# Attention scores on 32-row strips of TensorE with 0/1-masked keys, in a two-layer cross-attention and mixture-of-experts kernel

## The chip, the cores and the metric

The kernel runs on one core of a Trainium2 chip. A core has TensorE (PE: matmuls on an array of 128 rows by 128 columns; its loads of weights are shown apart, as PEld), VectorE (DVE), ScalarE (ACT), GpSimd (POOL), SyncE (SP, which here only issues DMAs), and 16 DMA engines. The metric is the device time of one execution in microseconds, as the median of three runs.

## The reference

The input x has 16 sequences of 128 tokens with 256 features; the context ctx has the same shape. Two layers follow each other, each an attention over the context and a mixture of experts, with a LayerNorm ahead of each:

```python
x = x + xattn0(layernorm(x), ctx)            # 16 heads of 16 features, rotary positions on q and k
x = x + ffn0(layernorm(x))                   # top 2 of 8 experts, and a shared one
x = x + xattn1(layernorm(x), ctx, mask)      # 16 heads of 16 features, padding mask on keys
x = x + ffn1(layernorm(x))                   # top 4 of 16 experts by groups, and a shared one
# each attention, for a sequence and a head h:
#   scores = q_h @ k_h.T / 4                 [128 x 128], contracted over 16 features
#   out_h  = softmax(scores (+ mask)) @ v_h
# then out = concat(out_h) @ Wo.T + bo
```

## The kernel before, in words

**Precision.** Products that must be accurate are made in three matmuls: each operand is split in a high and a low part (names with _hi and _lo, or index 0 and 1 in `k_parts` and `q_parts`), and hi x hi, lo x hi and hi x lo are summed in PSUM. ACT writes the high part as a rounded copy; DVE writes the low part as the value less its high part.

**Blocks.** Attention works on blocks `n` of four sequences (512 tokens), four blocks a layer. Within a block there are 16 groups of four heads: group i = (sequence b, g) with g from 0 to 3. All 16 groups go through one pipeline.

- PE, `scores` (L1341 to L1343, and L1348 for the mask in layer 1): 128 queries by 4 x 128 scores of a group, in one bank of PSUM. Bank g holds group g of a sequence.
- DVE, `shifted`: `nmax` (L1036), the negated maximum of each head's row, and for even g the subtraction (L1039) that makes `prob`. ACT: exp, L638 for even g from `prob`, L642 for odd g from the bank with `nmax` as bias, four instructions.
- PE, `turned` (L1358): four transposes of the probabilities. ACT `probT_hi` (L660), DVE `probT_lo` (L1065) split them.
- PE, `weighed` (L1373): probabilities times values, two parts. A column of ones beside the values gives the sums. DVE `rden` (L1045) inverts them, ACT `o_raw` (L650) copies the sums out of the bank, POOL (L461, L463, L466) adds the parts and multiplies by `rden` into `o_sb`. DVE does this for the last of a block (`last_outputs`).
- Ends of blocks: oT transposes (L1397), their split (ACT L674, DVE L1078), the products with Wo, and DVE's sum into `xres` (L1088).

The order is written out by hand: on PE, step i is scores(i+4), then turned(i), then weighed(i-2). In the last four steps of a block, where no scores are left, PE makes instead the projection units of the next block (`unit`, L1178): two of keys and two of queries, each 128 features by 512 tokens. Behind the steps PE makes the values of the next block, the oT transposes, the first four groups of scores of the next block, and the products with Wo. In layer 0 a unit goes on through DVE (L1009, twice: times cosine and times sine, with the bias), POOL `rotate` (L451), ACT (L624, high part) and DVE (`unit_low`, L1019, low part). In layer 1 it goes through ACT (L619, bias and scale), ACT (L624) and DVE (L1019). A unit needs the buffer `qk` that the unit two before it gives free.

**The keys.** A matmul here contracts over all 128 rows of the array, and a head has only 16 features. So the right-hand operand is `kexp`, a block-diagonal copy of the keys. It is 128 rows by four heads by 128 keys, where the rows of head j hold its keys in the columns of head j, and all else is zero. POOL sets it to zero once a layer, and SP's queue fills it in every block with small DMAs, of which each copies the 16 rows of a head. There are two buffers of `kexp`, used in turn by sequences:

```python
for g2 in range(2):
    for j in range(GRP):
        rows = slice(64 * g2 + HD * j, 64 * g2 + HD * (j + 1))
        src = k_parts[rows, :, :, b * S:(b + 1) * S]
        dst = kexp[b % 2][rows, :, g2::2, j, :]
        sp.dma_start(dst.bitcast(F32), src.bitcast(F32)).then_inc(a[f"kdma{b % 2}"], 16)
```

That is 8 DMAs a sequence, 32 a block, 256 in the program. SP issues them in order with the loads of the context; behind the last of layer 0 stand the fill of the sorted rows with zeros (L289, `sorted_x`, and L292, `summed`), and the loads of the expert weights (L295, `w_raw`), which POOL (L342) and others split.

The loops over blocks on PE and SP are hardware loops (`Fori`) over the first three blocks, with the fourth written out behind them.

## Time and profile before

| | |
|---|---|
| time, median of 3 runs | 1128.84 us (1124.97 to 1131.86) |
| span of the profiled execution | 1130.6 us; no time apart from it is given for that execution |
| PE busy | 990.0 us, 88% |
| DVE busy | 789.2 us, 70% |
| ACT busy | 588.3 us, 52% |
| POOL busy | 453.7 us, 40% |
| attention of layer 0 | from about 50 to 248 us |
| LayerNorm between attention and experts of layer 0 | 249 to 274 us |
| attention of layer 1 | 617 to 786 us |

The profile is of one execution. Busy shares are averages over stages with different limits, so they say where to look and not what sets the time. The chain of waits says that: it is followed back from the last instruction to what released each step. In a row with an idle time in brackets, the engine stood idle for so long before that instruction, and what is named released it.

### The profile page before, as it was taken

To read this page: it belongs to the slowest core of one execution; us is meant where nothing else is said; L and a number is where in the kernel's file an instruction comes from. 1 tells how busy PE (TensorE), PEld (TensorE's weight loads), DVE (VectorE), ACT (ScalarE), POOL (GpSimd) and SP (SyncE) were. 2 spreads that over 40 slices of the span, in tenths; PEclk is the share of its full clock that TensorE was granted. 3 is DMA by queue.
4 is the path that set the end of the run, shared out by engine and by line. 5 is a ranking of instruction groups with operands and counts; after the bars stand their busy time and mean duration, and the time that the engine had idled before them with its cause. 6 is when DMAs were issued, how large, how long until landed. Compare 5 with 4: busy or idle time off the path is not lost.

```text
span 1130.6 us, 20561 instructions
## 1 busy us (share of the span) xinstructions
PE 990.0 (88%) x6789; PEld 851.5 (75%) x6789; DVE 789.2 (70%) x1553; ACT 588.3 (52%) x1128; POOL 453.7 (40%) x481
## 2 busy tenths in 40 slices
PE   3798988957988999999946999995889999999995
PEld 2577776844868999999944777774678888888885
DVE  5587777856745677777746887885596766666665
ACT  5384655655423676666637877875622232232221
POOL 4384344424374566666651745342112112212210
PEclk9998989977989999999976999997799999999998
DMA  3311010291223788888760111010001000000002
GB/s 130 89 39 29 28 36 12 64 288 45 80 90 131 216 224 237 233 228 225 194 155 18 39 51 29 15 37 30 28 15 29 14 28 28 14 28 28 14 1 75
DMA packets 64609, 93.00 MB, mean 82 GB/s; under 512 B 8241, under 2 KB 51505, under 8 KB 64561
## 3 DMA queue, kind: packets, MB, share of 16 engines
q0 software_dynamic: 14784, 46.44, 14.8%
q1 hardware_dynamic: 49778, 45.97, 14.4%
q8 instruction: 25, 0.41, 0.2%
q14 instruction: 22, 0.18, 0.1%
HBM read 63.21 MB, written 20.79 MB: 74 GB/s over the span
## 4 chain that ended last, share of the span: by engine, by line
PE 46%; DVE 18%; ACT 13%; issue 10%; DMA 8%; POOL 3%; SPq 1%; ACTq 0%; DVEq 0%; POOLq 0%
PE bank L1178 28%; PE bank L1214 10%; DMA w_raw<-in_fw,w_idx 5%; DVE nmax L1036 4%; DVE probT_lo L1065 2%; DMA summed<-y_sb,tile_to 2%; DVE prob L1039 2%; PE bank L1273 2%; ACT probT_hi L660 2%; ACT xn L522 2%; ACT o_raw L650 2%; POOL qk L451 1%; POOL summed L404 1%; ACT w_hi L543 1%; DVE xres L957 1%
## 5 line engine op out<-in xcount | busy, mean ns | idle before, releaser
L1178 PE MATMUL bank<-xT_hi,w_hi 128*128 128x512 f32 x352 | 140.0, 398 | 3.2 <-DVE hid L970 2.2
L591 ACT ACTIVATE act_sb<-bank 128x512 f32<-128x512 f32 x88 | 52.6, 597 | 173.4 <-PE bank L1178 162.3
L1178 PE MATMUL bank<-xT_hi,w_lo 128*128 128x512 f32 x352 | 139.8, 397 | 1.7 <-issue 1.5
L1178 PE MATMUL bank<-xT_lo,w_hi 128*128 128x512 f32 x352 | 139.8, 397 | 1.1 <-issue 1.1
L970 DVE TENSOR_TENSOR hid<-bank,act_sb 128x512 f32<-128x512 f32 x88 | 60.8, 691 | 113.2 <-ACT act_sb L591 100.6
L342 POOL TENSOR_TENSOR w_hi<-w_raw,zero_col 128x768 fp32r<-128x768 f32 (+1 forms) x20 | 31.9, 1596 | 266.4 <-PE bank L1214 235.8
L957 DVE SCALAR_TENSOR_TENSOR xres<-bank,gate,xres 128x256 f32<-128x256 f32 x320 | 132.5, 475 | 0.8 <-PE bank L1214 0.8
L1178 PE MATMUL bank<-xsT_hi,w_hi 128*128 128x256 f32 x368 | 107.3, 291 | 2.3 <-DVE xsT_lo L924 1.5
L1214 PE MATMUL bank<-w_hi,hid_hi 128*128 128x256 f32 x352 | 100.0, 284 | 6.3 <-DVE hid_lo L978 6.2
L1065 DVE TENSOR_TENSOR probT_lo<-bank,probT_hi 128x512 f16<-128x512 f32 x128 | 87.9, 686 | 23.9 <-ACT probT_hi L660 23.2
L1178 PE MATMUL bank<-xsT_hi,w_lo 128*128 128x256 f32 x368 | 104.0, 283 | 0.0
L1178 PE MATMUL bank<-xsT_lo,w_hi 128*128 128x256 f32 x368 | 103.9, 282 | 0.0
L596 ACT ACTIVATE hid_hi<-hid 128x512 fp32r<-128x512 f32 x88 | 55.6, 632 | 91.9 <-PE bank L1214 53.7
L1214 PE MATMUL bank<-w_hi,hid_lo 128*128 128x256 f32 x352 | 99.2, 282 | 0.0
L1214 PE MATMUL bank<-w_lo,hid_hi 128*128 128x256 f32 x352 | 98.9, 281 | 0.0
L1358 PE MATMUL bank<-ident,prob 128*128 128x128 f32 x512 | 80.2, 280 | 14.4 <-ACT prob L638 7.7
L404 POOL DMA_INDIRECT summed<-y_sb,tile_to x46 | 83.9, 1824 | 21.5 <-DMA summed<-y_sb,tile_to 11.0
L1358 PEld LDWEIGHTS bank<-ident,prob 128*128 128x128 f32 x512 | 60.7, 143 | 37.6 <-ACT prob L638 20.8
L1036 DVE TENSOR_REDUCE nmax<-bank 128x4 f32<-128x512 f32 x128 | 85.5, 674 | 3.0 <-PE bank L1348 2.7
L369 POOL DMA_INDIRECT w_raw<-in_fw,w_idx x46 | 49.8, 1083 | 93.7 <-ACT y_sb L560 29.8
L543 ACT ACTIVATE w_hi<-w_raw 128x1536 fp32r<-128x1536 f32 x46 | 68.1, 1483 | 34.2 <-DMA w_raw<-in_fw,w_idx 33.9
L919 DVE TENSOR_TENSOR w_lo<-w_raw,w_hi 128x1536 fp32r<-128x1536 f32 x46 | 80.6, 1752 | 2.1 <-issue 1.4
(204 smaller groups left out, 2957.4 us busy)
## 6 DMA issues: line engine op xcount, KB each, us to landing
kexp<-k_parts SPq DMA_DIRECT2D x256, 32.0 KB, 2.0
w_raw<-in_fw SPq DMA_DIRECT2D x18, 384.0 KB, 3.0
sorted_x<-empty_row SPq DMA_DIRECT2D x2, 2967.0 KB, 20.6
xs<-sorted_x SPq DMA_DIRECT2D x23, 258.0 KB, 3.9
ctx_raw<-in_ctxT SPq DMA_DIRECT2D x8, 512.0 KB, 4.2
aw_raw<-in_aw SPq DMA_DIRECT2D x10, 256.0 KB, 3.2
summed<-empty_row SPq DMA_DIRECT2D x1, 2304.0 KB, 25.9
xres<-in_x SPq DMA_DIRECT2D x4, 512.0 KB, 6.2
```

What stands on the lines that cost most here:

```text
L404: nc.gpsimd.indirect_dma_start(out=summed, out_offset=bass.IndirectOffsetOnAxis(ap=tile_to[:, j, c:c + 1], axis=0), in_=y_sb[:, j % 2, c, ...
L543: nc.scalar.activation(w_hi4[s][:], w_raw4[s], ACT.Copy).then_inc(TS["w_hi"], 1)
L591: nc.scalar.activation(act_sb[:, (ls * J + j) % 2, :], bank[2 * ((ls * J + j) % 2) + 1][:], ACT.Silu).then_inc(f["act"], 1)
L596: nc.scalar.activation(hid_hi[:, ls % 2, j, :], hid[:, (ls * J + j) % 2, :], ACT.Copy).then_inc(f["hhi"], 1)
L919: nc.vector.tensor_tensor(w_lo4[s][:], w_raw4[s], w_hi4[s][:].bitcast(F32), ALU.subtract).then_inc(TS["w_lo"], 1)
L957: nc.vector.scalar_tensor_tensor(out=rows, in0=bank[4 + 2 * (ls % 2) + sub // 2][:, D * (sub % 2):D * (sub % 2 + 1)], scalar=gate[:, ds(it ...
L970: nc.vector.tensor_tensor(hid[:, r, :], bank[2 * r][:], act_sb[:, r, :], ALU.mult).then_inc(f["hid"], 1)
L1036: nc.vector.tensor_reduce(mx, grp, AX.X, ALU.max, negate=True).then_inc(a["max"], 1)
L1065: nc.vector.tensor_tensor(probT_lo[:, i % RINGT, :], bank[4 + i % 2][:], probT_hi[:, i % RINGT, :], ALU.subtract).then_inc(a["plo"], 1)
L1178: last = nc.tensor.matmul(dst, lh, rh, start=(i == 0), stop=(i == len(pairs) - 1))
L1214: last = nc.tensor.matmul(dst, h, w, start=(i == 0), stop=(i == len(pairs) - 1))
L1358: last = nc.tensor.transpose(bank[4 + i % 2][:, S * h:S * (h + 1)], prob[:, i % RING, S * h:S * (h + 1)], ident[:])
```

## The change

- `kexp`, its DMAs and its zeroing go. A tile `gap` stands in the place of `kexp`, so that the tiles behind it keep their addresses.
- `k_parts` holds each key unit twice for each part: once times `half_col[:, 0]` and once times `half_col[:, 1]`. `half_col` is 1 in the first or in the second 16 rows of every 32, and 0 elsewhere. DVE makes it once from the identity matrix. ACT and DVE thus write two copies of high and low part for each of two key units a block. The counts of the semaphores `qkhi` and `qklo` go from 4 to 6 a block.
- `scores` takes two groups at a time, g and g+1. A strip of 32 rows holds two heads of each of the two feature tiles u. A matmul contracts over the 32 rows of strip r, and its right-hand operand is the two masked copies side by side (256 columns). Bank r gets 256 columns for u = 0 and 256 for u = 1. Matmuls on the two strips alternate. The pair waits for the subtraction and the exp of the groups whose banks it writes.
- The heads of a group are now 8u + 2g + j; `weighed`, the outputs and `last_outputs` address them so (`four_by_two`).
- In layer 1 the mask is added by four matmuls of 256 columns over 32 rows, so `mask_b` and `first_row` stand on all strips. The DMA of the mask writes 128 partitions (1 MB) instead of one (8 KB).
- The `Fori` loops over blocks on PE and SP become Python loops, which are unrolled.

```diff
-        k_parts = sb(at, "k_parts", [P, 2, KT, N], F32R)
-
-        kexp = [sb(at, f"kexp{i}", [P, 2, NG, GRP, S], F32R) for i in range(2)]
+        k_parts = sb(at, "k_parts", [P, 2, KT, 2, N], F32R)
+        gap = sb(at, "gap", [P, 6 * 1024], F32)
...
-                sp.dma_start(mask_f, maskrow).then_inc(s_in, 16)
+                sp.dma_start(mask_f, maskrow.to_broadcast([P, TOK])).then_inc(s_in, 16)
...
-                with sp.Fori(0, NBLK - 1) as n:
+                for n in range(NBLK - 1):
                     sp.wait_ge(a["ctx_lo"], n + 1)
-                    sp.dma_start(ctx_raw[:], ctxT[:, :, ds(n * N + N, N)]).then_inc(a["ctx_in"], 16)
-                    keys(n)
-                keys(NBLK - 1)
+                    sp.dma_start(ctx_raw[:], ctxT[:, :, n * N + N:n * N + 2 * N]).then_inc(a["ctx_in"], 16)
...
-                    dst = k_parts if i < 2 else q_parts
-                    nc.scalar.activation(dst[:, 0, i % 2, :], qk[:, i % 2, :], ACT.Copy).then_inc(a["qkhi"], 1)
+                    if i >= 2:
+                        nc.scalar.activation(q_parts[:, 0, i % 2, :], qk[:, i % 2, :], ACT.Copy).then_inc(a["qkhi"], 1)
+                    else:
...
+                        for h in range(2):
+                            nc.scalar.activation(k_parts[:, 0, i, h, :], qk[:, i, :], ACT.Copy,
+                                                 scale=half_col[:, h:h + 1]).then_inc(a["qkhi"], 1)
...
+                    for h in range(2):
+                        dve.wait_ge(a["qkhi"], m * 6 + (2 * i + h + 1))
+                        nc.vector.scalar_tensor_tensor(
+                            out=k_parts[:, 1, r, h, :], in0=qk[:, r, :], scalar=half_col[:, h:h + 1],
+                            in1=k_parts[:, 0, r, h, :].bitcast(F32), op0=ALU.mult,
+                            op1=ALU.subtract).then_inc(a["qklo"], 1)
...
-                    if b >= 1 and g % 2 == 0:
+                    if b >= 1:
                         pe.wait_ge(a["sub"], n * 8 + (i - NG) // 2 + 1)
-                    elif b >= 1:
-                        pe.wait_ge(a["exp"], n * GROUPS + (i - NG + 1))
-                    if g == 0:
-                        pe.wait_ge(a[f"kdma{b % 2}"], n * 256 + (b // 2 + 1) * 128)
-                    q = [q_parts[:, part, g // 2, S * b:S * (b + 1)] for part in range(2)]
-                    k = [kexp[b % 2][:, part, g].rearrange("p h t -> p (h t)") for part in range(2)]
-                    nc.tensor.matmul(bank[g][:], q[0], k[0], start=True, stop=False)
-                    nc.tensor.matmul(bank[g][:], q[1], k[0], start=False, stop=False)
-                    last = nc.tensor.matmul(bank[g][:], q[0], k[1], start=False, stop=(l == 0))
...
+                        pe.wait_ge(a["exp"], n * GROUPS + (i + 1 - NG + 1))
+                    cols = slice(S * b, S * (b + 1))
+                    for u in range(KT):
+                        for part, (pq, pk) in enumerate(((0, 0), (1, 0), (0, 1))):
+                            for r in (g, g + 1):
+                                rows = slice(32 * r, 32 * r + 32)
+                                last = nc.tensor.matmul(bank[r][:, 256 * u:256 * u + 256], q_parts[rows, pq, u, cols],
+                                                        k_parts[rows, pk, u, :, cols], start=(part == 0),
+                                                        stop=(part == 2 and l == 0))
...
+                        if l == 1:
+                            at_tok = slice((n * BLK + b) * S, (n * BLK + b + 1) * S)
+                            for r in (g, g + 1):
+                                rows = slice(32 * r, 32 * r + 32)
+                                row = mask_b[rows, at_tok].unsqueeze(1).to_broadcast([32, 2, S])
...
                     for i in range(GROUPS):
                         if i + NG < GROUPS:
-                            scores(n, i + NG)
+                            if i % 2 == 0:
+                                scores(n, i + NG)
...
-                        for g in range(NG):
+                        for g in range(0, NG, 2):
                             scores(n + 1, g)
...
-                with pe.Fori(0, NBLK - 1) as n:
+                for n in range(NBLK - 1):
                     attend(n, True)
```

## Rows read from the trace of the kernel before

**Rows 1.** The page: busy time by engine, and the chain that ended last.

```profile
PE 990.0 (88%) x6789; PEld 851.5 (75%) x6789; DVE 789.2 (70%) x1553; ACT 588.3 (52%) x1128; POOL 453.7 (40%) x481
...
PE bank L1178 28%; PE bank L1214 10%; DMA w_raw<-in_fw,w_idx 5%; DVE nmax L1036 4%; DVE probT_lo L1065 2%; DMA summed<-y_sb,tile_to 2%; DVE prob L1039 2%; PE bank L1273 2%; ACT probT_hi L660 2%; ACT xn L522 2%; ACT o_raw L650 2%; POOL qk L451 1%; POOL summed L404 1%; ACT w_hi L543 1%; DVE xres L957 1%
```

**Rows 2.** Windows: us, busy of PE, PEld, DVE, ACT, POOL, clock, DMA, GB/s.

```profile
87.60:138.70 51.10, 44.76 (x344) 37.21 (x344) 39.09 (x69) 30.50 (x73) 23.25 (x33) 0.93 0.12 31
645.50:687.10 41.60, 39.61 (x337) 31.04 (x337) 34.28 (x61) 32.99 (x78) 18.23 (x29) 1.00 0.15 38
```

**Rows 3.** Chain of waits in a block of layer 0: start, us, step.

```profile
122.03 0.50 ACT probT_hi L660
...
125.69 0.49 ACT probT_hi L660
```

**Rows 4.** Timeline of PE, then DVE, in the same block of layer 0.

```profile
120.42 0.47 PE L1341 MATMUL bank<-kexp,q_parts 128*128 128x512 f32 x1
...
120.97 0.40 PE L1343 MATMUL bank<-kexp,q_parts 128*128 128x512 f32 x1
...
125.38 0.63 PE L1358 MATMUL bank<-ident,prob 128*128 128x128 f32 x4 [0.38 <-ACT prob L638]
...
123.27 0.64 DVE L1036 TENSOR_REDUCE nmax<-bank 128x4 f32<-128x512 f32 x1
...
126.21 0.69 DVE L1065 TENSOR_TENSOR probT_lo<-bank,probT_hi 128x512 f16<-128x512 f32 x1 [0.38 <-ACT probT_hi L660]
```

**Rows 5.** Timeline of PE, two products of 256 columns in a row.

```profile
104.60 0.28 PE L1178 MATMUL bank<-aw_hi,oT_hi 128*128 128x256 f32 x1
...
104.72 0.28 PE L1178 MATMUL bank<-aw_hi,oT_lo 128*128 128x256 f32 x1
```

**Rows 6.** Timeline of PE, then DVE, at a block's head in layer 1.

```profile
664.08 0.40 PE L1341 MATMUL bank<-kexp,q_parts 128*128 128x512 f32 x1
...
665.20 0.69 DVE L1036 TENSOR_REDUCE nmax<-bank 128x4 f32<-128x512 f32 x1
...
668.41 0.68 DVE L1036 TENSOR_REDUCE nmax<-bank 128x4 f32<-128x512 f32 x1
```

**Rows 7.** Timeline of ACT and DVE at the start of layer 0.

```profile
55.80 1.14 ACT L642 ACTIVATE prob<-bank,nmax 128x128 f32<-128x128 f32 x4
...
57.00 1.28 DVE L1036 TENSOR_REDUCE nmax<-bank 128x4 f32<-128x512 f32 x2
```

**Rows 8.** Timeline of PE and DVE at the start of layer 1.

```profile
622.41 0.50 PE L1341 MATMUL bank<-kexp,q_parts 128*128 128x512 f32 x1 [1.04 <-DMA kexp<-k_parts]
...
623.64 0.69 DVE L1036 TENSOR_REDUCE nmax<-bank 128x4 f32<-128x512 f32 x1 [1.10 <-PE bank L1348]
```

**Rows 9.** Timeline of POOL and DVE in the LayerNorm after attention 0.

```profile
256.78 2.75 POOL L342 TENSOR_TENSOR w_hi<-w_raw,zero_col 128x1536 fp32r<-128x1536 f32 x1 [17.22 <-DMA w_raw<-in_fw]
...
257.40 2.14 DVE L767 SCALAR_TENSOR_TENSOR shift<-meanvar,rstd 128x4 f32<-128x4 f32 x1
```

**Rows 10.** Timeline of DVE in the key units of layer 0.

```profile
134.21 0.69 DVE L1019 TENSOR_TENSOR k_parts<-qk,k_parts 128x512 fp32r<-128x512 f32 x1 [1.47 <-ACT k_parts L624]
134.82 0.75 DVE L1009 SCALAR_TENSOR_TENSOR qk<-bank,bias_col,rope_tab 128x512 f32<-128x512 f32 x1
```

**Rows 11.** Timeline of ACT at the end of a block, layer 1.

```profile
646.59 0.63 ACT L624 ACTIVATE k_parts<-qk 128x512 fp32r<-128x512 f32 x1
647.12 0.49 ACT L650 ACTIVATE o_raw<-bank 128x400 f32<-128x400 f32 x1
...
649.79 0.60 ACT L660 ACTIVATE probT_hi<-bank 128x512 f16<-128x512 f32 x1 [0.28 <-PE bank L1358]
```

**Rows 12.** Windows of 2 us ahead of `values`, columns as in the second group.

```profile
92.00:94.00 2.00, 0.36 (x8) 0.28 (x8) 1.59 (x3) 1.26 (x3) 0.97 (x2) 0.99 0.21 50
94.00:96.00 2.00, 0.92 (x11) 0.93 (x12) 1.13 (x3) 0.00 (x0) 0.72 (x2) 0.50 0.21 49
...
652.00:654.00 2.00, 1.15 (x24) 0.99 (x21) 1.37 (x4) 1.97 (x5) 1.37 (x3) 1.00 0.15 36
```

More of the change, by code:

```diff
@@ L212, in tile_no, with four_by_two @@
             return it * (STEPS * J) + (ls * J + j)
+        def four_by_two(c):
+            return (o_raw[:, c % 2].rearrange("p (u m) w -> p u m w", u=2),
+                    o_sb[:, c // 2].rearrange("p (u c m) d -> p c u m d", u=2, c=2)[:, c % 2])
         block = ctx.enter_context(nc.Block())
@@ L262, in _ @@
                     later_constants()
-                def keys(n):
-                    sp.wait_ge(a["qklo"], n * 4 + 2)
-                    for b in range(BLK):
-                        if b >= 2:
-                            sp.wait_ge(a["score"], n * GROUPS + (b - 1) * NG)
-                        for g2 in range(2):
-                            for j in range(GRP):
-                                rows = slice(64 * g2 + HD * j, 64 * g2 + HD * (j + 1))
-                                src = k_parts[rows, :, :, b * S:(b + 1) * S]
-                                dst = kexp[b % 2][rows, :, g2::2, j, :]
-                                sp.dma_start(dst.bitcast(F32), src.bitcast(F32)).then_inc(a[f"kdma{b % 2}"], 16)
-                sp.wait_ge(a["kzero"], 2)
-                with sp.Fori(0, NBLK - 1) as n:
+                for n in range(NBLK - 1):
                     sp.wait_ge(a["ctx_lo"], n + 1)
-                    sp.dma_start(ctx_raw[:], ctxT[:, :, ds(n * N + N, N)]).then_inc(a["ctx_in"], 16)
-                    keys(n)
-                keys(NBLK - 1)
+                    sp.dma_start(ctx_raw[:], ctxT[:, :, n * N + N:n * N + 2 * N]).then_inc(a["ctx_in"], 16)
                 if l == 0:
@@ L458, in outputs @@
                                 rotate(n + 1, i)
[L459 removed]
+                        raw, dst = four_by_two(c)
                         pool.wait_ge(a["ocopy"], n * 8 + (c + 1))
[L461 removed]
+                        nc.gpsimd.tensor_tensor(dst, raw[:, :, :, 0:16], raw[:, :, :, 18:34], ALU.add).then_inc(a["oadd"], 1)
                         pool.wait_ge(a["oadd"], n * 14 + (2 * c + 1))
[L463 removed]
+                        nc.gpsimd.tensor_tensor(dst, dst, raw[:, :, :, 34:50], ALU.add).then_inc(a["oadd"], 1)
                         pool.wait_ge(a["oadd"], n * 14 + (2 * c + 2))
                         pool.wait_ge(a["rden"], n * 8 + (c + 1))
[L466 removed]
+                        nc.gpsimd.tensor_tensor(dst, dst, rden[:, c % 2].rearrange("p (u m) -> p u m", u=2).unsqueeze(3).to_broadcast([P, 2, 4, HD]),
                                                 ALU.mult).then_inc(a["o"], 1)
                 nc.gpsimd.memset(v_parts[:, :, :, HD:HD + 2], 1.0).then_inc(a["vones"], 1)
[L470 to L471 removed]
                 if l == 0:
@@ L1350, in scores @@
-                    last.then_inc(a["score"], 1)
+                        pe.wait_ge(a["exp"], n * GROUPS + (i + 1 - NG + 1))
[7 more added lines that the diff above has]
+                                                        stop=(part == 2 and l == 0))
+                                if u == KT - 1 and part == 2 and l == 0:
+                                    last.then_inc(a["score"], 1)
+                        if l == 1:
[3 more added lines that the diff above has]
+                                row = mask_b[rows, at_tok].unsqueeze(1).to_broadcast([32, 2, S])
+                                last = nc.tensor.matmul(
+                                    bank[r][:, 256 * u:256 * u + 256].rearrange("p (h t) -> p h t", h=2),
+                                    first_row[rows, :], row, start=False, stop=True)
+                                if u == KT - 1:
+                                    last.then_inc(a["score"], 1)
@@ L1374, in weighed @@
                                                     p[:, i % RINGT, S * h:S * (h + 1)],
-                                                    v_parts[:, b, GRP * g + h, :], start=(part == 0), stop=(part == 1))
+                                                    v_parts[:, b, head, :], start=(part == 0), stop=(part == 1))
                     last.then_inc(a["pv"], 1)
@@ L1431, in _ @@
                     pe.wait_ge(s_vset, 2)
-                pe.wait_ge(s_set, 5)
-                for g in range(NG):
+                pe.wait_ge(s_set, 7)
+                for g in range(0, NG, 2):
                     scores(0, g)
-                with pe.Fori(0, NBLK - 1) as n:
+                for n in range(NBLK - 1):
                     attend(n, True)
```

67 lines of the change are left out of this document (34 added, 33 removed).

## The prediction

> **What bounds the kernel now.** I read the page first, then the two attention loops by windows, then the chain of waits inside one block of each, and last the timelines of PE, DVE, ACT and SP where the change touches them. The page [rows 1] shows PE 88% busy and lines of PE at the head of the chain, and that invites one to expect a gain from faster score matmuls. But most of PE's chain is L1178 and L1214, the FFN, which the change does not touch. What the change is worth must be read inside attention, some 190 us of layer 0 and 170 us of layer 1. A middle block takes 51.1 us in layer 0 and 41.6 us in layer 1 [rows 2].
>
> In the body of a block the chain has no PE step: ACT copies probT_hi, DVE makes probT_lo, rden, nmax and the shifted prob, ACT makes exp and o_raw and copies the next probT_hi. This ring turns once for two groups, from 122.03 to 125.69 [rows 3]: 3.66 us, and the same in layer 1. PE in that time does two score groups, two sets of transposes and two of weighed sums. In layer 0 it then idles 0.38 us before it can transpose, and DVE idles 0.38 us for ACT [rows 4]; a score group takes PE 0.31+0.23+0.23 = 0.77 us. In layer 1 the mask matmul adds 0.23 us and PE is full, though not in the ring. What the change speeds up is thus beside the path.
>
> **Part 1: the scores.** Before, two groups are 6 matmuls of 512 columns: 2 x 0.77 = 1.5 us. After, they are 12 matmuls of 256 columns. A 256-column matmul steps by 0.12 us [rows 5]. If two strips don't overlap at all, a pair takes 12 x 0.12 = 1.4 us; if they overlap fully, 0.7 us. In layer 1 the masks are 2 x 0.23 before and 4 x 0.12 or half of it after: a pair is 1.9 or 0.95 us with them. No row of before shows two strips. I take full overlap (a strip leaves the other rows of the array idle) and keep the other end. In the ring it matters little: the group that PE scores from 120.42 on is read by DVE at 123.27 [rows 4], 2.8 us later, and either pair is done before that: 0 us at either end.
>
> The Trainium skill (TensorE: Matmul & The Clock Gate, Part 3: Packing small matmuls) has tiles in different row groups run at the same time, 3.07 times faster for four tiles; by it the pair is near 0.7 us. No row of before shows this. Against the change the skill says (TensorEngine Tiling (Array Packing), Key Properties) that a change of tiling mode drains TensorE. No row shows that either; its result is the rival "PE becomes the limit".
>
> The order changes too: a pair is ready only when both groups are, and it waits for the exp of both groups in whose banks it writes. Where that can show is the head of a block. In layer 1 DVE comes to the loop's first nmax at 665.10 and starts it at 665.20, after one score group of 0.94 us that began at 664.08 [rows 6]. With overlap the pair takes the same 0.95 us: 0. Without it a pair ends 0.9 us late: 3 blocks x 0.9 = +2.7 us, the upper end. Layer 0 has no masks and 0.9 us of slack in this place: 0. At the start of layer 0 the pair waits for an exp that ended at 56.9, while DVE wanted its scores at 57.6 [rows 7]: 56.9 + 0.7 to 1.4 of scores + 0.16 of tail, +0.5 us (0.2 to 0.9).
>
> **Part 2: the DMAs of keys.** 256 issues of about 0.6 us on SP go, with their queue. They end two waits at the start of layer 1: the second held PE 1.04 us until 622.41, and DVE lost 1.10 us before the nmax at 623.64 [rows 8]. The new order still waits there for the exp of group 1 (ended 621.8). I count -0.5 us, between -1.6 and +0.7. Elsewhere no wait on these DMAs stands on the chain. SP is freed: the zero fill of sorted_x and summed (SP L289, L292, from 222.9 to 240.4) goes out about 100 us sooner, so the weights that SP asks for at 248.9 do not queue behind it. POOL began to split them at 256.78, and DVE's shift, 0.16 us elsewhere, took 2.14 us beside that split [rows 9] and 2.75 beside the next. The split moves perhaps 3.5 us forward and will meet other shifts of the same LayerNorm. I count 0, between -4.6 (both waits gone) and +2.5 (one more). The wider mask DMA (1 MB for 8 KB) is issued at 32.2 and read by DVE at 51.6, and L986 stays at its 1.20 us by its columns: 0. The removed memsets ran in idle POOL time: 0.
>
> **Part 3: two masked copies of the keys.** This is the price. For each of two key units, ACT L624 and DVE L1019 now run twice. One more DVE operation is 0.61 us in step (134.21 to 134.82) [rows 10], and 0.06 more as scalar_tensor_tensor, since L1009 of that form takes 0.75 for the 0.69 of tensor_tensor; the first of the two gains the 0.06 too.
> Layer 0: the unit chain goes DVE qk and rope_b, POOL qk (1.28), ACT k_parts, DVE k_parts, then DVE qk of the next unit, which starts as k_parts gives way. DVE idled 1.47 us [rows 10] waiting inside this chain, so nothing hides the second operation: 0.67 + 0.06 = 0.7 us a unit, 1.4 us a block (1.2 to 1.7, the top if POOL's o_sb operations at 134.65 are in DVE's way). Queued behind are unit_build of the next unit, rden, and POOL's rotate for it. Four builds (one ahead of the loop, three in it): 5.6 us.
> Layer 1: ACT is nearly full in the same place, and a copy is 0.53 us in step (646.59 to 647.12) [rows 11]. Two more are 1.07 us, less the 0.28 us that ACT idles: 0.8 us a block. Late is then probT_hi of group 15, with it the last weighed sum, values and the output. DVE has idle time for its part. Three builds in the loop: 2.4 us. The one ahead of it is hidden: ACT idled 1.45 us before the q unit at 611.39.
> Half_col's reduction runs in DVE's idle 1.20 us before 32.97: 0. If everything here were hidden, Part 3 would be 0; if nothing were, 4 x 1.7 + 3 x 1.1 = 10 us.
>
> **Part 4: unrolled loops on PE and SP.** The same instructions without branches, PE not in the ring: 0.
>
> **Sum.** 5.6 + 2.4 + 0.5 - 0.5 = +8.0 us. It stands against the profiled span, 1130.6, which is 1.8 us above the median of the runs, 1128.84, inside their own spread of 7 us. On the median: 1137.
>
> **Rivals.**
> *Cheap copies (0.22).* Half of Part 3 hides, since DVE idles right there, and Part 2 gives its 1.6 in full: 4 - 1.6 + 0.5 = +3: 1132, no measurable change. Against it: DVE idles because it stands in that chain, in order.
> *PE does gate the ring (0.10; the other side).* In layer 1 PE has no idle time in the body. If the waits between DVE and ACT really come from PE, the ring falls to DVE's own work, 3.66 - 0.38 = 3.28 us: 0.38 x 5 turns x 8 blocks = 15 us less: 1122. It decides from 14 us of gain on. Against it: layer 0 turns in the same 3.66 us with PE idle.
> *The clock (0.10).* Less work on PE can lower its clock. Its granted clock is 0.50 (1.2 GHz) from 94 to 100 us, after PE was busy 0.36 us of 2, and `values` then takes 5.31 us; in layer 1 it keeps 1.00 (2.4 GHz) with 1.15 us of 2 busy [rows 12], and `values` takes 2.96. Part 3 lengthens that idle time. A fall there costs 2.4 x 3 = 7 us, and as much again if the units of layer 0 meet it: 1144 to 1151.
> *PE becomes the limit (0.10).* No overlap, and a drain on either side of the pair, sized as a matmul's tail (0.39 long, 0.23 in step: 0.16). Layer 1 then needs PE for 3.3 + 0.3 = 3.6 us of the 3.66: the ring stands, but in the head of each block, where DVE turns in 3.2 us (665.20 to 668.41) [rows 6], it loses 0.4 x 2, with the 0.9 of Part 1: 4 x 1.7 = +7 on top: 1144.
> *Weight loads are laid bare (0.06).* The LDWEIGHTS before these matmuls last 0.19 us each by their rows of the timeline and were hidden; there are now twice as many. At 0.19 a matmul a pair is 2.3 us, layer 1 goes to 4.0 us a turn: 0.37 x 7 x 4 = +10: 1147. At 0.3 (load, then matmul) both layers are PE's, 1.2 and 1.7 us a turn: +80: 1217.
>
> **How the numbers follow.** The forecast, slower by Part 3, has 0.42; its own range is 1132 to 1142. About 0.5%, 5.6 us, is what a measurement of this kernel can tell from no change. Slower: 0.37 of the forecast + 0.10 + 0.10 + 0.06 = 0.63. No change: 0.22 + 0.05 of the forecast = 0.27. Faster: 0.10. The range takes in 1122 on the one side and the clock's 1151 on the other: 1121 to 1152. Outside are loads laid bare beyond 0.2 us and larger gains or clock losses, under 0.2.
>
> **What will show it.** After the change: no kexp rows; score matmuls of 32 rows and 256 columns, two of them starting almost together if strips overlap; the ring still 3.66 us a turn in both layers; more than 0.38 us of PE idle before its transposes; middle blocks of 52.5 and 42.4 us; twice as many L624 and L1019 rows for keys. The prediction is wrong if the ring gets shorter (PE did gate it), if PE has no idle time in layer 0 (strips or loads cost), if the granted clock in the bodies or at `values` of layer 1 drops to 0.50, or if blocks keep their length (the copies hid).

## The result, and the profile after

The changed kernel takes 1149.45 us (median of 4 runs, 1148.25 to 1151.33), the kernel before 1127.2 us (4 runs, 1124.97 to 1131.86). The ratio is 1.0186, with a 95% interval of 1.0158 to 1.0215: 21 us slower (22 between the medians). The forecast was 1137, its range ended at 1152; the direction was right and the size was less than half of what came.

The page of the changed kernel (busy time by engine, chain that ended last) answers to [rows 1]:

```profile
PE 962.9 (84%) x7237; PEld 850.1 (74%) x7237; DVE 801.1 (70%) x1570; ACT 598.0 (52%) x1144; POOL 438.2 (38%) x479
...
PE bank L1184 28%; PE bank L1220 8%; PE bank L1279 3%; DVE nmax L1039 3%; DMA w_raw<-in_fw,w_idx 3%; DVE probT_lo L1068 2%; DVE prob L1042 2%; ACT probT_hi L654 2%; POOL sorted_x L374 2%; ACT o_raw L644 2%; DMA summed<-y_sb,tile_to 2%; POOL qk L441 2%; ACT xn L510 1%; POOL summed L393 1%; PE bank L1369 1%
```

PE has 27 us less to do and DVE 12 us more. The page says no more than that. Where the time went is read from milestones. I take DVE's sums into `xres`, one pair for each block (L1088 before, L1091 after). The first middle block of each kernel's layer 0 lies between these rows, first before, then after:

```profile
L1088 DVE TENSOR_TENSOR xres<-bank,xres x2: 681/682/682, 107.8 to 108.4; 128x512 f32 x2
L1088 DVE TENSOR_TENSOR xres<-bank,xres x2: 680/680/681, 158.9 to 159.5; 128x512 f32 x2
```

```profile
L1091 DVE TENSOR_TENSOR xres<-bank,xres x2: 680/680/680, 112.0 to 112.6; 128x512 f32 x2
L1091 DVE TENSOR_TENSOR xres<-bank,xres x2: 680/680/680, 166.1 to 166.7; 128x512 f32 x2
```

Laid end to end, the same rows give this ledger of the two profiled executions:

| stretch | before, us | after, us | more |
|---|---|---|---|
| start to the first `nmax` of layer 0 | 53.8 | 55.6 | 1.8 |
| its first block, to `xres` | 54.0 | 56.4 | 2.4 |
| its two middle blocks | 51.1, 51.1 | 54.1, 54.5 | 6.4 |
| its last block | 38.2 | 38.1 | -0.1 |
| experts of layer 0 and start of layer 1 | 370.4 | 368.8 | -1.6 |
| first block of layer 1, from its first `nmax` | 45.0 | 47.4 | 2.4 |
| its other blocks | 41.5, 41.6, 39.5 | 42.0, 43.4, 39.2 | 2.0 |
| experts of layer 1, to the end | 344.4 | 347.2 | 2.8 |
| sum | 1130.6 | 1146.7 | 16.1 |

The profiled execution of before lies above its median. The stage that varies is the experts of layer 0 with the start of layer 1 behind them: in the kernel before with one loop unrolled (below) it took 364.5 us for these 370.4, while every other stretch agreed within 0.6. So a few microseconds there tell nothing, and the -1.6 is no finding. The middle blocks repeat to some tenths in nearly all executions. The starts of the layers do so less well: the start took 52.8 to 54.3 us in the kernel before and its variants below, and the first block of layer 1 took 48.8 us in a variant of the changed kernel with the same attention (47.4 here). So a difference of a microsecond in those rows is not a finding either.

Windows of the changed kernel's middle blocks, two of each layer, answer to [rows 2] (us, busy time and count of PE, PEld, DVE, ACT, POOL, granted clock, DMA share, GB/s):

```profile
112.00:166.10 54.10, 44.19 (x396) 38.74 (x395) 40.56 (x72) 31.88 (x76) 23.43 (x33) 0.84 0.69 171
...
674.90:716.90 42.00, 34.39 (x406) 29.88 (x404) 35.50 (x65) 34.15 (x80) 18.24 (x29) 1.00 0.05 14
716.90:760.30 43.40, 35.69 (x405) 31.18 (x403) 35.49 (x64) 34.05 (x80) 18.80 (x29) 0.96 0.01 1
```

The clock is 0.84 in a middle block of layer 0 where it was 0.93. Windows of 3 us inside that block show where:

```profile
121.00:124.00 3.00, 1.51 (x23) 1.24 (x21) 2.25 (x6) 3.00 (x10) 2.73 (x2) 1.00 0.00 0
124.00:127.00 3.00, 3.00 (x27) 2.68 (x27) 2.58 (x5) 2.44 (x7) 1.49 (x4) 0.55 0.65 156
127.00:130.00 3.00, 3.00 (x31) 2.81 (x31) 2.96 (x6) 2.37 (x7) 0.66 (x3) 0.50 0.39 145
130.00:133.00 3.00, 3.00 (x29) 2.65 (x26) 2.59 (x5) 2.48 (x7) 1.20 (x3) 0.50 1.05 348
133.00:136.00 3.00, 3.00 (x18) 2.47 (x16) 1.50 (x4) 2.04 (x7) 1.26 (x3) 0.74 1.11 281
```

From 124 to 134.5 us, in the body of the block, the granted clock is 0.50 (1.2 GHz). Before the change it stood at 1.00 in that body, from 108 to 143 us. The ring of DVE and ACT does not feel it: `prob` (L1042) starts at 128.11 and at 131.77, still 3.66 us a turn. What feels it is the first key unit behind the ring. The timeline of PE, then of DVE:

```profile
133.73 0.63 PE L1184 MATMUL bank<-ctx_hi,aw_lo 128*128 128x512 f32 x1
...
134.81 0.40 PE L1184 MATMUL bank<-ctx_hi,aw_lo 128*128 128x512 f32 x1
...
134.65 0.19 DVE L1048 RECIPROCAL rden<-o_raw 128x8 f32<-128x8 f32 x1
136.84 0.75 DVE L1002 SCALAR_TENSOR_TENSOR qk<-bank,bias_col,rope_tab 128x512 f32<-128x512 f32 x1 [1.99 <-PE bank L1184]
...
140.41 1.42 DVE L1020 SCALAR_TENSOR_TENSOR k_parts<-qk,half_col,k_parts 128x512 fp32r<-128x512 f32 x2 [1.56 <-ACT k_parts L617]
```

Before, DVE started this unit at 130.73, right behind `rden`. Now it waits 1.99 us. Counted from the `xres` of the block, PE began the unit 1.3 us later than before (133.16, for 127.72 before), and then took 3.48 us for 2.81, since the clock came back only during the unit. Then come the masked copies, as forecast: from the first unit's `qk` (136.84) to that of the third (151.78) it is 14.94 us for 13.35 (130.73 to 144.08), +1.6. From there to the next `xres` the block gains 0.5 us: the second fall of the clock, at `values`, now ends inside that stage (158.4 us), which takes 4.84 us for 5.27. 1.95 + 1.6 - 0.5 = 3.1 us is the longer block. The zero fill, which now runs beside the block (DMA share 0.69), is not the reason for its length: the second middle block has a DMA share of 0.00, the same fall of the clock (179 to 190 us) and 54.4 us.

### The profile page after: what moved, and what is told of

Same layout as the page of the kernel before. It is cut to its first block, busy times and chain, and to the rows that moved or that the text cites. A ratio compares the mean times of both kernels' runs of the same rounds, so it can differ in the third digit from the quotient of the medians.

```text
span 1146.7 us, 21018 instructions
## 1 busy us (share of the span) xinstructions
PE 962.9 (84%) x7237; PEld 850.1 (74%) x7237; DVE 801.1 (70%) x1570; ACT 598.0 (52%) x1144; POOL 438.2 (38%) x479
## 4 chain that ended last, share of the span: by engine, by line
PE 44%; DVE 20%; ACT 13%; issue 11%; DMA 6%; POOL 5%; DVEq 0%; ACTq 0%; POOLq 0%
PE bank L1184 28%; PE bank L1220 8%; PE bank L1279 3%; DVE nmax L1039 3%; DMA w_raw<-in_fw,w_idx 3%; DVE probT_lo L1068 2%; DVE prob L1042 2%; ACT probT_hi L654 2%; POOL sorted_x L374 2%; ACT o_raw L644 2%; DMA summed<-y_sb,tile_to 2%; POOL qk L441 2%; ACT xn L510 1%; POOL summed L393 1%; PE bank L1369 1%
## 5 line engine op out<-in xcount | busy, mean ns | idle before, releaser
L579 ACT ACTIVATE act_sb<-bank 128x512 f32<-128x512 f32 x88 | 52.6, 598 | 167.8 <-PE bank L1184 167.7
L1369 PE MATMUL bank<-ident,prob 128*128 128x128 f32 x512 | 88.0, 302 | 35.8 <-DVE probT_lo L1068 27.2
L654 ACT ACTIVATE probT_hi<-bank 128x512 f16<-128x512 f32 x128 | 77.2, 603 | 12.4 <-PE bank L1369 11.9
```

Of the source, the lines that this page charges most:

```text
L579: nc.scalar.activation(act_sb[:, (ls * J + j) % 2, :], bank[2 * ((ls * J + j) % 2) + 1][:], ACT.Silu).then_inc(f["act"], 1)
L654: nc.scalar.activation(probT_hi[:, i % RINGT, :], bank[4 + i % 2][:], ACT.Copy).then_inc(a["phi"], 1)
L1369: last = nc.tensor.transpose(bank[4 + i % 2][:, S * h:S * (h + 1)], prob[:, i % RING, S * h:S * (h + 1)], ident[:])
```

## The experiments

Eleven kernels were run. Where part of the computation is left out, the text says so. All ratios are to the kernel before, timed on the same chip.

**Twice the scores.** The first question was the clock: would more work for PE make the kernel faster?

```diff
-                    for u in range(KT):
+                    for again in range(2):
+                      for u in range(KT):
                         for part, (pq, pk) in enumerate(((0, 0), (1, 0), (0, 1))):
...
```

> The changed kernel with every score matmul of a pair issued twice: the second pass starts the banks afresh, so the result is the same and PE only has more to do (24 matmuls of 256 columns and 32 rows for 12). Clock theory (the loss beyond the masked copies comes from TensorE falling to 1.2 GHz in the body of a block, because the scores keep it less busy): the granted clock stays at 1.00 through the bodies, a middle block of layer 0 takes 52.5 us for 54.3, and the time falls by 5 to 10 us below the changed kernel's 1149, although work was added. Rival 'strips are dear' (drain, bare loads, or PE the limit): twice the matmuls make it slower, 1155 or more. Rival 'copies are dearer than priced': no change, 1147 to 1151.

Measured: ratio 1.0236 (1.0217 to 1.0255), for 1.0186 of the changed kernel. The time went the way of the rival, slower; the blocks went the way of the clock theory. A middle block of layer 0 takes 52.0 us, with the clock at 0.97 over it and at 1.00 in its body:

```profile
116.50:168.50 52.00, 44.84 (x492) 39.95 (x490) 40.49 (x72) 31.82 (x76) 23.22 (x33) 0.97 0.73 179
```

```profile
138.61 0.69 DVE L1068 TENSOR_TENSOR probT_lo<-bank,probT_hi 128x512 f16<-128x512 f32 x1 [0.38 <-ACT probT_hi L654]
139.22 0.19 DVE L1048 RECIPROCAL rden<-o_raw 128x8 f32<-128x8 f32 x1
139.47 0.75 DVE L1002 SCALAR_TENSOR_TENSOR qk<-bank,bias_col,rope_tab 128x512 f32<-128x512 f32 x1
```

DVE starts the unit right behind `rden`: the 1.99 us of waiting are gone, and the ring has its old 0.38. The loss came elsewhere. The first blocks of both layers run at 0.50 at their start in the changed kernel already (to 66 us, and from 630 to 640 us) and grew by 4.5 us (layer 0, with its start) and 2.6 us (layer 1, 50.0 us). Layer 1's blocks grew from 42.0 to 44.3 us: 0.8 us in their heads, where DVE waits for the longer scores, and 1.5 us at `values`, where the clock now fell and which took 4.46 us for 2.95. Their ring kept its 3.67 us, so PE did not become its limit.

The run also prices a strip. Timeline of PE, two lines in a row:

```profile
73.92 1.69 PE L1348 MATMUL bank<-k_parts,q_parts 32*128 32x256 f32 x24
75.55 0.66 PE L1370 MATMUL bank<-ident,prob 128*128 128x128 f32 x4
```

24 matmuls keep PE 1.63 us and 12 keep it 0.90 (next experiment), so twelve more cost 0.73 us, 0.061 each. That is half the 0.12 us step of [rows 5]: two strips in turns overlap fully. The other 0.17 us comes once a pair.

**One strip after the other.**

```diff
-                    for u in range(KT):
-                        for part, (pq, pk) in enumerate(((0, 0), (1, 0), (0, 1))):
-                            for r in (g, g + 1):
+                    for r in (g, g + 1):
+                        rows = slice(32 * r, 32 * r + 32)
+                        for u in range(KT):
+                            for part, (pq, pk) in enumerate(((0, 0), (1, 0), (0, 1))):
...
```

> The changed kernel with the six matmuls (and two mask matmuls) of one strip ahead of those of the other, instead of taking turns. Clock theory: if turns are what makes strips overlap, a pair takes 1.4 us instead of 0.8, PE is as busy as before the change and keeps its clock, and the time falls by 5 to 10 us to about 1142. If the strips overlap in any order, nothing changes (1149). Rival 'strips are dear': fewer switches between strips, so faster too, but then with the clock unchanged and PE less busy. Rival 'copies are dearer': no change.

Measured: ratio 1.0385 (1.0365 to 1.0405). A miss, and the most telling one. The timeline of PE, first with turns (the changed kernel), then without:

```profile
66.50 0.98 PE L1347 MATMUL bank<-k_parts,q_parts 32*128 32x256 f32 x12
67.40 0.66 PE L1369 MATMUL bank<-ident,prob 128*128 128x128 f32 x4
```

```profile
125.65 1.31 PE L1347 MATMUL bank<-k_parts,q_parts 32*128 32x256 f32 x12
126.89 0.66 PE L1364 MATMUL bank<-ident,prob 128*128 128x128 f32 x4
```

A pair keeps PE 0.90 us with turns and 1.24 without, so the turns matter. But PE, now busier, did not keep its clock. Windows of layer 1:

```profile
706.40:709.40 3.00, 2.67 (x34) 2.26 (x29) 2.25 (x4) 3.00 (x8) 2.43 (x2) 1.00 0.00 0
709.40:712.40 3.00, 2.75 (x21) 2.56 (x22) 2.66 (x6) 2.43 (x7) 1.51 (x4) 0.57 0.50 142
```

It fell after PE had been busy 2.67 of 3 us, where in the kernel before it had stood at 1.00 with 2.06 of 3 in the same layer (684.60 to 687.60). Nor did it come back soon: from 642 to 675 us it stood at 0.50 with PE drawn as busy all the time, of which two windows:

```profile
645.00:648.00 3.00, 3.00 (x17) 2.54 (x16) 2.23 (x4) 2.49 (x7) 3.00 (x2) 0.50 0.00 0
669.00:672.00 3.00, 3.00 (x18) 2.55 (x17) 2.16 (x4) 1.04 (x4) 0.84 (x2) 0.50 0.00 0
```

So PE's busy time, as the profile draws it, does not order these stretches. The first block of layer 1 took 60.3 us, the next two 48.

**One masked copy** (the second head of a strip gets scores from the wrong keys).

```diff
-                        for h in range(2):
-                            nc.scalar.activation(k_parts[:, 0, i, h, :], qk[:, i, :], ACT.Copy,
-                                                 scale=half_col[:, h:h + 1]).then_inc(a["qkhi"], 1)
+                        nc.scalar.activation(k_parts[:, 0, i, 0, :], qk[:, i, :], ACT.Copy,
+                                             scale=half_col[:, 0:1]).then_inc(a["qkhi"], 2)
...
-                    for h in range(2):
+                    for h in range(1):
...
```

> The changed kernel with only the first masked copy of each key unit made (one ACT and one DVE instruction a unit instead of two); scores read it for both heads of a strip, so the second head's scores are left out (they come from the wrong keys). My step on the copies: 1.4 us a block less in layer 0, 0.8 in layer 1, 1149 - 6 to 8 = 1141 to 1143, and the clock still falls in the bodies. Rival 'copies are dearer than priced, and the clock is harmless': the middle blocks return to 51.1 us and the time to 1128 to 1133.

Measured: ratio 1.0087 (1.0058 to 1.0117), between the two forecasts: middle blocks of layer 0 at 51.2 and 51.1 us, of layer 1 at 41.1. Windows of its first middle block:

```profile
117.30:120.30 3.00, 3.00 (x26) 2.71 (x27) 2.96 (x5) 2.92 (x7) 0.00 (x0) 0.50 0.03 5
120.30:123.30 3.00, 3.00 (x26) 2.65 (x25) 2.25 (x6) 3.00 (x9) 2.75 (x2) 0.50 0.00 0
123.30:126.30 3.00, 3.00 (x30) 2.81 (x30) 2.60 (x5) 2.33 (x6) 1.37 (x4) 0.50 0.59 152
126.30:129.30 3.00, 3.00 (x47) 2.67 (x44) 2.96 (x6) 2.41 (x7) 0.72 (x2) 0.99 0.37 136
```

The clock falls here too, but some 7 us earlier in the block, and it is back before the key unit at 134.44: no cost. So from this run alone the copies look dearer (3 us a block) than they are. The chain from the first to the third unit gives back 1.0 us of it (13.90 for 14.94). Of the other 2, 1.7 lie ahead of the first unit and are the clock's fall, moved to a place where it costs nothing. The price of the new chain is the +1.6 of the timeline, which the doubled scores show as well, with no fall of the clock near it (139.47 to 154.42, 14.95 us): 1.0 for the second copies and 0.55 that stay with one copy, most of it because the masked operations are longer (ACT 0.72 us for 0.63, DVE 0.75 for 0.69). In layer 1 a middle block gives back 0.8 us (41.1 for 42.0) and is then shorter than before the change (41.5).

**PE's loop unrolled in the kernel before.**

```diff
-                with pe.Fori(0, NBLK - 1) as n:
+                for n in range(NBLK - 1):
                     attend(n, True)
```

> The kernel before with only PE's loop over blocks unrolled. My step: 0, the time of before (1127) within 0.3%. Rival 'the unrolled code is what costs' (instruction fetch of PE): slower by more than 4 us, with the loss in the expert stages too, where the changed kernel's cycle of 24 matmuls took 4.25 us for 4.21.

Measured: 0.9993 (0.9981 to 1.0005). Unrolling PE's loop costs nothing that shows; SP's was not tried.

**The place of the tiles.** In the experts of layer 1, which the change does not touch, the chain showed a cycle of 24 matmuls in 4.219 us in the two kernels without strips and in 4.247 in the four with them. The change puts one small tile, `half_col`, ahead of most others. Two runs tried that from both sides:

```diff
-        half_col = sb(ctx, "half_col", [P, 2], F32)
+        half_col = sb(ctx, "half_col", [P, 16], F32)[:, 0:2]
```

> The changed kernel with half_col padded from 8 to 64 bytes a partition, so that the tiles behind it (the expert weights among them) keep their offsets of before modulo 64 bytes instead of lying 8 bytes further. Theory 'offset' (the 8 bytes make matmuls on those tiles slower: a cycle of 24 matmuls took 4.247 us in the experts of layer 1 in every kernel with the strips, 4.219 in the two without): the cycle returns to 4.219, 64 cycles give 1.8 us, and about as much may come from layer 0's experts and the projections; 2 to 5 us faster than the changed kernel (about 1.0186 times before). Rival 'something else of the change' (PE's tiling mode, its code): the cycle stays at 4.247, no change.

```diff
         mask_b = sb(ctx, "mask_b", [P, B * S], BF16)
+        shift8 = sb(ctx, "shift8", [P, 2], F32)
```

> The kernel before with an unused tile of 8 bytes a partition in the place of half_col. Theory 'offset': the cycle of 24 matmuls takes 4.247 us for 4.219, and the time rises by 2 to 5 us, ratio 1.002 to 1.004. Rival: no change, cycle 4.219.

Measured: 1.0142 (1.0110 to 1.0174) for the padded changed kernel, 1.0019 (0.9996 to 1.0041) for the kernel before with an 8-byte tile. The chains in the experts, first of the kernel before with the 8 bytes, then of the padded changed kernel (start, us, step):

```profile
1090.68 2.81 PE bank L1179 x12
1093.49 1.44 PE bank L1215 x12
```

```profile
1090.69 2.76 PE bank L1184 x12
1093.46 1.44 PE bank L1220 x12
```

The unused 8 bytes alone bring the 2.81; the padding brings 2.76, less than the 2.78 to 2.80 of the kernel before. So the place is shown for the cycle. For the whole time it is not: the interval of the kernel with 8 bytes takes in 1, and those of the changed kernel with and without padding overlap. From `xres` to the end the padded kernel takes 342.7 us and the changed kernel 347.2, but the kernel before with 8 bytes, with the same cycle as the changed one, takes 345.7. What it is about the place that does this was not tried.

**Work on all rows as filler.** Four matmuls ahead of each pair, on all 128 rows, into the bank that the pair then starts afresh:

```diff
                     cols = slice(S * b, S * (b + 1))
+                    if b >= 1:
+                        for fill in range(4):
+                            nc.tensor.matmul(bank[g][:, 0:256], q_parts[:, 0, fill % 2, cols],
+                                             k_parts[:, 0, fill % 2, :, cols], start=True, stop=True)
```

> The changed kernel with four matmuls of 128 rows and 256 columns ahead of each pair of score groups inside a block (their results are overwritten by the pair). They use all rows of the array, where the score matmuls use 32, and cost PE about 0.5 us a pair. Clock theory, sharpened by the first four runs (what keeps the clock is work on all rows; matmuls of 32 rows one strip at a time lost it with PE busy 2.67 of 3 us): no fall in the bodies of either layer, middle blocks of layer 0 at 52.0 to 52.5 for 54.3, layer 1's at 41.8 with none of the 44.3 of the doubled scores; 5 to 7 us faster than the changed kernel, a ratio of 1.012 to 1.014 to before. Rival 'PE's time is what counts' (the scores or their switches set the pace): slower, as with the doubled scores, 1.022.

Measured: 1.0181 (1.0148 to 1.0214), no better than the changed kernel. The middle blocks of layer 0 came out as expected (52.0 and 52.6 us, 4 us together), but the first blocks grew by 1.6 us (with the start of layer 0) and 2.9 us (layer 1), and layer 1's other blocks stayed (42.1 and 43.7). Not all of that growth need be the filler's, since the padded kernel without it is 0.9 and 1.4 us longer there too. Four fillers kept PE 1.13 us where the clock was 0.50 (59.46 to 60.58) and 0.65 us where it was 1.00. So the next kernel has the padding, and the filler only where the fall costs something (`if l == 0 and n >= 1 and b >= 1`):

> The changed kernel with half_col padded, and the four full-row matmuls ahead of a pair only in layer 0 and only from the second block on (with them everywhere, the first block of each layer, which runs at 1.2 GHz, became longer by 1.6 and 2.9 us, and layer 1's later blocks gained nothing). Clock theory: middle blocks of layer 0 at 52.0 and 52.6 us for 54.3 and 54.6, all else as in the padded kernel (ratio 1.0142): 4 us less, ratio 1.010 to 1.011, although PE does more. Rival 'the fills only move the loss': 1.014 or more.

Measured: 1.0100 (1.0070 to 1.0131), as expected. The windows of its two middle blocks of layer 0:

```profile
112.70:164.70 52.00, 42.69 (x418) 37.22 (x416) 40.45 (x73) 31.88 (x76) 23.12 (x33) 0.97 0.70 178
164.70:217.40 52.70, 43.75 (x418) 38.48 (x416) 40.58 (x73) 31.94 (x76) 24.02 (x33) 0.94 0.01 1
```

It issues 72 matmuls more than the changed kernel with the padding and takes about 4 us less. It is the best version of the change, and still slower than the kernel before.

**All three at once** (the second heads' scores are left out).

```diff
+                    if b >= 1:
+                        for fill in range(4): ...
...
+        half_col = sb(ctx, "half_col", [P, 16], F32)[:, 0:2]
...
+                    for h in range(1):
```

> The changed kernel with all three at once: four full-row matmuls ahead of each pair, half_col padded to 64 bytes, and only one masked copy of each key unit (the second head's scores are left out: they come from the wrong keys). If the three terms (clock, offset, copies) are the whole of the loss, this is the time of before within 0.4%: ratio 0.997 to 1.004. If another term is missing (the pair's waits, the freed queue, the wider mask), it stays above 1.005.

Measured: 1.0084 (1.0057 to 1.0111), above 1.005: another term is missing. By its ledger it is 3.3 us late at the first `xres` and loses 2.1 us in the first block of layer 1 (47.1 for 45.0), while its middle blocks are those of before (51.3 and 50.9, 41.3). What is missing shows in the first blocks, though the fillers there may be a part of it. Its profiled execution is 4 us below its median, so not all of the 0.84% is in this ledger.

**Fewer scores, on all rows** (the kernel before without the products with low parts, so with less precise scores).

```diff
-                    nc.tensor.matmul(bank[g][:], q[0], k[0], start=True, stop=False)
-                    nc.tensor.matmul(bank[g][:], q[1], k[0], start=False, stop=False)
-                    last = nc.tensor.matmul(bank[g][:], q[0], k[1], start=False, stop=(l == 0))
+                    last = nc.tensor.matmul(bank[g][:], q[0], k[0], start=True, stop=(l == 0))
```

> The kernel before with one of the three score matmuls of a group instead of three (the products with the low parts are left out, so scores are less precise): two groups take PE about 0.6 us, less than a pair of the changed kernel (0.9), but on all 128 rows. Clock theory as first stated (PE's busy time): the clock falls in the bodies of layer 0 as in the changed kernel, and middle blocks take 53 us. Clock theory as sharpened (work on few rows does not keep the clock): it stays at 1.00 there and blocks stay at 51.1 us. Rival of the prediction 'PE gates the ring': blocks get shorter, 2 us or more each.

Measured: 0.9971 (0.9953 to 0.9988), and blocks of 51.0 us. Its windows in the first middle block of layer 0:

```profile
107.80:110.80 3.00, 1.16 (x13) 0.85 (x13) 2.96 (x6) 2.03 (x6) 0.00 (x0) 1.00 0.00 0
110.80:113.80 3.00, 2.16 (x26) 1.71 (x26) 2.96 (x5) 2.55 (x8) 0.00 (x0) 1.00 0.14 33
113.80:116.80 3.00, 1.36 (x15) 0.97 (x15) 2.33 (x5) 3.00 (x8) 1.36 (x1) 1.00 0.22 54
116.80:119.80 3.00, 2.21 (x26) 1.59 (x26) 2.85 (x6) 2.43 (x7) 2.20 (x4) 1.00 0.12 36
```

PE is busy 1.16 and 1.36 of 3 us, less than in any window of the changed kernel's body there, and the clock stays at 1.00. But it does so in this block only. The head of the same block and that of the next, where PE does the same work, first and second:

```profile
107.00:110.00 3.00, 0.53 (x5) 0.44 (x5) 2.96 (x5) 2.11 (x5) 0.17 (x1) 1.00 0.05 12
110.00:113.00 3.00, 2.11 (x27) 1.51 (x25) 2.96 (x6) 2.55 (x7) 0.00 (x0) 1.00 0.09 21
```

```profile
158.00:161.00 3.00, 0.55 (x4) 0.52 (x4) 2.97 (x6) 2.03 (x6) 0.00 (x0) 0.86 0.05 11
161.00:164.00 3.00, 3.00 (x27) 2.64 (x26) 2.97 (x5) 2.63 (x7) 0.00 (x0) 0.57 0.03 6
```

The clock was low in the second (from 160.5 to 163.6 us), and again in the last block at 211 us, and in the first at 68 us, after PE had been busy 1.40 of 3 us on 128-row work. The second middle block lost no length by it (51.0 us, and 50.9 for the first). So neither form of the clock theory is shown: work on all rows does not always keep the clock, and the same work kept it in one block and lost it in the next. And the doubled scores, whose added work is all on 32 rows, kept it in the bodies of layer 0. What stands is what the edits did: in the middle blocks of layer 0 the changed kernel lost the clock in the body both times, and the kernels with more matmuls there (doubled scores, fillers) did not.

The run also settles the rival of the other sign: with two thirds of the score matmuls gone, the ring still turns in 3.66 us (`nmax` to `nmax`, 121.66 to 125.32). PE never gated it. It did cost something in the heads of layer 1's blocks: a block there takes 41.1 us for 41.5.

**The padding in the kernel before.**

```diff
         mask_b = sb(ctx, "mask_b", [P, B * S], BF16)
+        pad64 = sb(ctx, "pad64", [P, 16], F32)
```

> The kernel before with an unused tile of 64 bytes a partition in the place of half_col. In the padded changed kernel the expert cycle of 24 matmuls took 4.200 us, in the kernel before 4.219, with an 8-byte tile in it 4.247. Theory 'place' (the cycle follows from where the tiles behind lie): 4.200 here too, 1.2 us less in layer 1's experts and perhaps as much elsewhere: ratio 0.997 to 0.999 to before, a version faster than both. Rival 'the 4.200 is owed to the other changes': 4.219 and ratio 1.000.

Measured: cycle 4.200 us as expected (its rows of 12 matmuls take 2.76, like those of the padded changed kernel), and 0.9986 (0.9967 to 1.0005): perhaps 1.6 us, not shown to be faster.

## Why the prediction was right and where it failed

**The ring: right, and the step that failed.** 3.66 us a turn in both kernels, with PE out of it. The step "either pair is done before that: 0 us at either end" is right for the ring, and it is the step that failed for the block. It asked only when PE is done, and not what a lighter PE does to its own clock. The fall in the body costs 1.95 us in each middle block of layer 0 at the first key unit, and I had no term for it in the sum. Two more terms were put at nothing: first blocks, 2.7 us beyond their copies, and the place of the tiles.

**The head of layer 1's blocks: put at 0, a gain.** Before, the chain there ran through PE: the products with Wo that DVE sums into `xres`, then the first score group. With lighter scores both come sooner. Timeline of DVE, before ([rows 6] has its next line), then after:

```profile
663.58 1.52 DVE L1088 TENSOR_TENSOR xres<-bank,xres 128x512 f32 x2
```

```profile
674.90 1.28 DVE L1091 TENSOR_TENSOR xres<-bank,xres 128x512 f32 x2
676.09 0.68 DVE L1039 TENSOR_REDUCE nmax<-bank 128x4 f32<-128x512 f32 x1
```

The `nmax` starts 1.62 us behind `xres` before and 1.19 after: 0.4 us less a block.

**The clock as a rival: right cause, mostly in another place.** I gave it 0.10 and looked at `values`, behind a longer idle time. In layer 0 the trace shows no loss there but a gain of 0.5 us a block; the fall that costs comes in the body. In layer 1 it came at `values` once, in the third block, which took 4.44 us there for 2.95:

```profile
750.00:753.00 3.00, 3.00 (x19) 3.00 (x18) 1.77 (x5) 0.64 (x1) 0.86 (x4) 0.60 0.00 0
```

That the measured 1149 lies in this rival's 1144 to 1151 is luck: its price was 7 us for layer 1's `values`, and as much again for the units of layer 0, and the clock is seen to cost 4.3 us of the 22 at those two. The Trainium skill (TensorE: Matmul & The Clock Gate, Part 1: The HAM clock gate) has the clock follow how busy PE has been. The kernel with fewer scores agrees (falls after 1.40 and 0.55 of 3 us busy, though 0.53 kept it a block earlier), and so do the doubled scores and the fillers. The strips in series do not: busy 2.67 of 3 us ahead of a fall, and 3.00 of 3 through 33 us at 0.50.

**Scores: right, but for a fixed part.** Full overlap is what twelve more matmuls show: 0.73 us for my 0.7. A pair takes 0.90, since 0.17 us comes once a pair. Before, the first matmul of each group took 0.31 us for 0.23 [rows 4], 0.16 for two groups, so a drain beyond that does not show; the gap ahead of a pair is about 0.1 us. The Trainium skill (TensorE: Matmul & The Clock Gate, Part 3: Packing small matmuls) has 3.07 for four tiles; for two strips the runs show 0.12 / 0.061 = 2.0 in the steps, and 1.24 / 0.90 = 1.4 for a pair in series against one in turns.

**Copies: right.** 1.6 us a block in layer 0 for a forecast of 1.4. In layer 1 the kernel with one copy shows 0.8 (42.0 and 41.1), as forecast; the block is only 0.5 longer than before, since its head gained 0.4. With the 1.8 us ahead of the first scores the net is 1.8 + 3 x 1.6 + 3 x 0.5 = 8.1 us. That this is my 8.0 is partly luck: the copies alone come to 9.1, and the 1.8 is from a stretch that varies by more than a microsecond.

**The start of layer 0: size off by half a microsecond.** DVE waited for the second pair of scores, which had waited for an exp, and was then made at 1.2 GHz. Timeline of DVE, answering to [rows 7]:

```profile
58.83 0.68 DVE L1039 TENSOR_REDUCE nmax<-bank 128x4 f32<-128x512 f32 x1
60.56 0.69 DVE L1039 TENSOR_REDUCE nmax<-bank 128x4 f32<-128x512 f32 x1 [1.05 <-PE bank L1347]
```

**The DMAs of keys and the zero fill: no term of them shows.** PE's wait for a DMA in [rows 8] is gone, but DVE now waits 1.53 us for PE where it had waited 1.10, and the first block of layer 1 is 2.4 us longer. Its pair starts at 630.85, waits as at the start of layer 0, and runs at 0.50, where before the change the clock stood at 1.00 through the first block:

```profile
633.00:636.00 3.00, 3.00 (x18) 2.57 (x20) 2.68 (x5) 1.60 (x3) 3.00 (x2) 0.50 0.00 0
```

That points to the clock in the first blocks too, but no run separates it from the pair's wait. The first block has no time of its own for this in my sum.

**The tiles' place: a term that was missing.** The diff says that `gap` keeps the addresses; `half_col` does not. In the experts of layer 1 the cycle accounts for 64 x 0.028 = 1.8 of the 2.8 us of the ledger. Padding took the ratio from 1.0186 to 1.0142, some 5 us, with intervals that overlap.

**The sum again.** Copies 8.1 as above; clock in the two middle blocks of layer 0 (1.95 - 0.5) x 2 = 2.9; first blocks beyond their copies 0.8 + 1.9 = 2.7; the third block of layer 1, with its `values` at the low clock, 1.4 more; experts of layer 1, 2.8. Together 17.9, against 17.7 for all stretches but the one that varies by itself. The medians differ by 22; the rest is the height of the profiled execution of before, and perhaps what the shifted tiles cost in the stretch that varies. How these share it stays open. Open too is what decides a fall: why it comes in the third block of layer 1 and not in the second, or in the head of one block and not of another with the same work.

## What to carry to other kernels

Before an engine off the critical path is made lighter, ask what its idle time does to itself: here the freed PE dropped to half its clock, and the next piece of work on the path was on PE. A matmul on a part of the array's rows may save time and still lose the clock, which later full-size matmuls then pay. And a new tile, however small, can move its neighbours and their speed with it; padding did not bring the old cycle back (4.200 us for 4.219), so the check is the old kernel with the same tile added.

## What the runs showed of the hardware that I had not expected

- With 32-row matmuls in series the granted clock fell to 0.50 after PE had been busy 2.67 of 3 us, and stood at 0.50 for 33 us with PE busy 3.00 of 3.
- In the kernel with fewer scores the same PE work kept the clock at 1.00 in the head of one block (107 to 113 us) and lost it in the next (161 to 164 us).
- The same 24 matmuls took 4.247, 4.219 or 4.200 us with an unused or padded tile of 8, 0 or 64 bytes a partition ahead of their operands. One kernel with the 8 bytes and the filler gave 4.233, so the place is not all of it.
- Two strips taken in turns: 12 matmuls of 32 rows and 256 columns in 0.90 us, 24 in 1.63 us, so 0.061 us a matmul where one of 128 rows steps by 0.12; in series 12 take 1.24 us.
